# Six transformer layers after a new table of times: a quarter of a layer between the two samples, query shifts in four groups, high and low parts transposed together

## The reference, cut to what matters

```
for i in range(6):
    xn = _adaln(x, noise_emb, n1_w[i], n1_b[i])            # layer norm, gain and shift from the noise embedding
    q, k, v = split(xn @ qkv_w[i].T);  q = _rope(q); k = _rope(k)
    x = x + _attn(q, k, v, src_mask) @ so_w[i].T           # softmax(q k^T / sqrt(8)) v, 512 x 512 per head
    xn = _adaln(x, noise_emb, n2_w[i], n2_b[i])
    q = _rope(xn @ cq_w[i].T); k = _rope(context @ ck_w[i].T); v = context @ cv_w[i].T
    x = x + _attn(q, k, v, ctx_mask) @ co_w[i].T           # 512 x 77 per head
    xn = _adaln(x, noise_emb, n3_w[i], n3_b[i])
    x = x + gelu(xn @ f1_w[i].T + f1_b[i]) @ f2_w[i].T + f2_b[i]
```

## Time and profile before

| | us |
|---|---|
| median of 3 runs (4430.06 to 4431.96) | 4431.53 |
| the profiled execution | 4427.45 |
| its span | 4425.7 |
| of the span: ahead of the six layers | 2869.9 |
| the six layers, first `mean` to last `fres` | 1386.7 |
| behind them | 169.0 |

### The profile page before, as it was taken

How to read it: one execution, slowest core, us unless ns; L and a number is a source line. 1 busy time by engine, 2 the same in 40 slices (tenths; PEclk the granted TensorE clock), 3 DMA queues, 4 the chain that set the end, 5 groups by cost and what they waited for, 6 DMA issues and landing times. The chain is left out here.

```text
span 4425.7 us, 67855 instructions
## 1 busy us (share of the span) xinstructions
PE 3717.7 (84%) x19183; PEld 2083.4 (47%) x19244; DVE 2774.0 (63%) x13500; ACT 2297.4 (52%) x6560; POOL 660.9 (15%) x2307
## 2 busy tenths in 40 slices
PE   7888888888888888888899999678888888888768
PEld 2366667666766666666333333223333333333222
DVE  3457777777777777777544544466666666666534
ACT  5356666666666666666433334135555555555433
POOL 0322222222222222222320000210000000000002
PEclk9999999999999999999999999578888888888879
DMA  0100000000000000000110000011111111111000
GB/s 9 58 1 1 1 1 1 1 2 1 1 1 1 1 1 2 1 1 1 36 38 1 1 1 22 17 59 45 58 47 62 49 61 48 59 46 46 27 27 5
DMA packets 48773, 93.56 MB, mean 21 GB/s; under 512 B 11296, under 2 KB 31792, under 8 KB 48144
## 3 DMA queue, kind: packets, MB, share of 16 engines
q1 hardware_dynamic: 48400, 89.22, 6.2%
HBM read 72.88 MB, written 15.39 MB: 20 GB/s over the span
## 5 line engine op out<-in xcount | busy, mean ns | idle before, releaser
L2250 ACT ACTIVATE t_ex<-ps 128x1024 f32<-128x1024 f32 (+1 forms) x480 | 472.1, 1021 | 572.0 <-PE ps L2197 558.4
L923 PE MATMUL ps<-g_dh,w_p 128*128 128x77 f32 x2032 | 453.0, 304 | 341.0 <-DVE g_dh L1014 341.0
L931 PE MATMUL ps<-g_dh,w_p 128*128 128x128 f32 x4064 | 662.6, 285 | 0.0
L2345 DVE TENSOR_REDUCE t_ncol<-ps 128x1 f32<-128x512 f32 x768 | 486.4, 682 | 157.8 <-PE ps L2170 157.0
L923 PEld LDWEIGHTS ps<-g_dh,w_p 128*128 128x128 f32 x2032 | 302.1, 188 | 535.5 <-DVE g_dh L1014 535.5
L988 DVE SCALAR_TENSOR_TENSOR g_used<-g_encg,g_e 128x77 f32<-128x77 f32 x3072 | 549.7, 229 | 0.0
L931 PEld LDWEIGHTS ps<-g_dh,w_p 128*128 128x128 f32 x4064 | 535.1, 191 | 0.0
L940 PE MATMUL ps<-g_th,g_vrep 128*128 128x77 f32 x2048 | 453.8, 303 | 0.0
L958 ACT ACTIVATE g_th<-ps 128x77 f32<-128x77 f32 x1024 | 242.4, 237 | 400.8 <-PE ps L923 400.8
L935 PE MATMUL ps<-g_dh,g_uhh 128*128 128x129 f32 x2032 | 437.0, 297 | 0.0
L997 DVE TENSOR_REDUCE g_ntop<-ps 128x1 f32<-128x77 f32 x1024 | 243.0, 237 | 260.4 <-PE ps L940 248.3
(11 more groups left out here) (483 smaller groups left out, 5439.1 us busy)
## 6 DMA issues: line engine op xcount, KB each, us to landing
t_qst<-t_turn_q SPq DMA_DIRECT2D x288, 96.0 KB
t_kst<-t_turn_k SPq DMA_DIRECT2D x144, 96.0 KB
t_turn_q<-t_part SPq DMA_DIRECT2D x24, 384.0 KB, 2.5
t_turn_k<-t_part SPq DMA_DIRECT2D x12, 384.0 KB, 3.3
t_wf<-in_t_wf SPq DMA_DIRECT2D x6, 514.5 KB, 5.7
m_experts<-in_experts SPq DMA_DIRECT2D x1, 3072.0 KB, 11.9
t_wa<-in_t_wa SPq DMA_DIRECT2D x6, 448.0 KB, 3.5
t_wx<-in_t_wx SPq DMA_DIRECT2D x6, 448.0 KB, 4.5
```

Source lines behind the costliest of these rows:

```text
L923: M(att[c], w["att_h"], moved(c, t, S), start=False, stop=True, skip_group_check=True).then_inc(*st.sem("att", c))
L931: return M(gates[c][:, g], w["uh"][:, g * D:(g + 1) * D], moved(c, t, SPAN), start=False, stop=False, skip_group_check=True)
L2250: A(ex[0:kw, slot[pf, c, l, n]], ps[0:kw, at:at + 2], ACT.Exp, scale=SCALE).then_inc(*st.sem(f"{pf}e{n}", c))
L2345: V.tensor_reduce(ncol[:, c, n % TT, n // TT:n // TT + 1], ps[:, at], AX, ALU.max, negate=True)\
```

## The change

There are two tables, one for each lane, with new times; a layer is due every 207.24 us and lane 1 comes 52.59 us behind lane 0. High and low parts share a tile (`nhl`), are transposed by one step `tr` and copied by one step `rc`; the shift rows of self attention go in four groups of 4 heads. A reader's time in the choice of PSUM banks is no longer 1.0 us but by its kind, and a slot of `ex` is chosen as the one due free first. Semaphores are kept per lane in two objects. Cut to its core:

```diff
-    LAYER, LAG = 209.87, 104.92
-    TABLE = {
-            "s a": [24.99, 25.21, 25.56, ... 95.17],
-            "s b": [70.18, 71.46, ... 121.77],
-            "x a": [153.28, ... 158.94],   "x res": [188.99],   "f fres": [208.94],
-            "s rows": [66.72, 100.26],
+    LAYER, LAG = 207.24, 52.59
+    TABLE = ({                                # lane 0
+            "s a": [26.5, 27, ... 89.37],
+            "s b": [46.73, 48.47, ... 105.26],
+            "x mean": [115.65],  "x a": [141.35, ... 160.14],  "f mean": [187.69],  "f fres": [206.44],
+            "s kt": [16.1],  "s qt": [17.4],  "s kl": [19.9, 26.2, 30.4, 34.6],  "s ql": [22, 24.1, 28.3, 32.5],
+            "s rows": [43.51, 57.45, 81.13, 93.44],  "load": [58.59],
+        }, {                                  # lane 1
+            "s a": [37.43, 38.99, ... 97.96],
+            "s b": [58.46, 59.18, ... 113.5],
+            "x mean": [125.98],  "x a": [146.84, ... 159.59],  "f mean": [185.21],  "f fres": [204.88],
+            ...
+        })
-        nhi, nlo = sb("nhi", [P, B, TT, H3], BF16), sb("nlo", [P, B, TT, H3], BF16)
-        nrow = sb("nrow", [H3, B, 2, T], BF16)
+        nhl = sb("nhl", [P, B, TT, 2 * H3], BF16)
+        nrow = sb("nrow", [2 * H3, B, 2, T], BF16)
+        HELD = {"m": 0.75, "e": 1.1, "g": 3.4}
-                until[j], holder[j] = when[reader, pf, c, l, rn] + 1.0, (pf + name, c, l)
+                until[j], holder[j] = when[reader, pf, c, l, rn] + HELD.get(reader, 0.8), (pf + name, c, l)
-        slot = {e: i % EXR for i, e in enumerate(exps)}
+        for e in exps:
+            i = min(range(EXR), key=lambda i: slot_until[i])
+            slot[e], slot_held[e] = i, slot_holder[i]
+            slot_until[i], slot_holder[i] = when["o", e[0], e[1], e[2], e[3] // 2] + 1.15, e
-                    sp.wait_ge(*st.at(f"{pf}rhi{n}", c, l))
-                    sp.wait_ge(*st.at(f"{pf}rlo{n}", c, l))
-                    hs = 8 * n if pf == "s" else 0
-                    nh = 8 if pf == "s" else H3
+                    sp.wait_ge(*st[c].at(f"{pf}rc{n}", 0, l))
+                    hs, nh = (4 * n, 4) if pf == "s" else (0, H3)
                     for i in range(2):
-                        sp.dma_start(qst[SHIFT_ROW + i:SHIFT_ROW + i + 1, c, hs:hs + nh], nrow[0:nh, c, i]).then_inc(shifted[pf, c], 16)
+                        sp.dma_start(qst[SHIFT_ROW + i:SHIFT_ROW + i + 1, c, hs:hs + nh], nrow[nh * i:nh * i + nh, c, n % 2])\
+                            .then_inc(shifted[pf, c], 16)
-                elif what in ("thi", "tlo"):
+                elif what == "tr":
+                    pe.wait_ge(*st[c].at(f"{pf}lo{n}", 0, l))
+                    hs, nh = (8 * n, 8) if pf == "s" else (0, 2 * H3)
                     for t in range(TT):
+                        mm = M(ps[0:nh, at, t * P:(t + 1) * P], nhl[:, c, t, hs:hs + nh], identb[:], start=True, stop=True)
-                    if pf == "s" and n % 16 == 0:
-                        pe.wait_ge(shifted["s", c], 16 * (4 * l + 2 * (n // 16) + 2))
+                    if pf == "s" and n % 8 == 0:
+                        pe.wait_ge(shifted["s", c], 16 * (8 * l + 2 * (n // 8) + 2))
                     elif what == "q1":
-                        dve.wait_ge(*st.at(pf + "qr", c, l))
-                        V.tensor_copy(q1, qr).then_inc(*st.sem(pf + "q1", c))
+                        dve.wait_ge(*st[c].at(pf + "qr", 0, l))
+                        V.tensor_copy(q1, qr).then_inc(*st[c].sem(pf + "q1"))
-                    dve.wait_ge(*st.at(f"{pf}m{32 * n + 31 if pf == 's' else H3 // 2 - 1}", c, l))
+                    dve.wait_ge(*st[c].at(f"{pf}m{16 * n + 15 if pf == 's' else H3 // 2 - 1}", 0, l))
+                elif what == "rc":
+                    nh = 8 if pf == "s" else 2 * H3
+                    dve.wait_ge(*st[c].at(f"{pf}tr{n}", 0, l))
+                    if n >= 2:
+                        dve.wait_ge(shifted["s", c], 16 * (8 * l + 2 * (n - 1)))
+                    V.tensor_copy(nrow[0:nh, c, n % 2], ps[0:nh, bank("tr", pf, c, l, n)]).then_inc(*st[c].sem(f"{pf}rc{n}"))
```

More of the change, by code:

```diff
@@ new lines, in transformer3_stage @@
+    LAYER, LAG = 207.24, 52.59
+    TABLE = ({
[34 rows of a table added]
+            },
+            "act": {
+                "s sq": [1.1],
+                "s rstd": [2.88],
+                "s e": [47.45, 49.19, 50.93, 52.66, 54.4, 57.57, 59.31, 63.68, 65.42, 68.22, 71.84, 72.92, 74.66, 76.4, 78.75,
+                    80.49, 85.96, 87.04, 88.12, 89.2, 90.31, 91.86, 92.94, 94.02, 96.9, 97.98, 99.06, 100.14, 101.23, 103.02,
+                    104.1, 105.98],
+                "s og": [82.93, 108.21],
+                "s inv": [84.71, 109.99],
+                "x sq": [116.75],
+                "x rstd": [120.22],
+                "x e": [168.35, 169.43, 170.98, 172.06, 174.28, 175.83, 176.91, 179.2],
+                "x og": [175.25, 181.43],
+                "x inv": [177.95, 183.52],
+                "f sq": [188.79],
+                "f rstd": [190.57],
+                "f g": [197.71],
+            },
+            "dve": {
[36 rows of a table added]
+            },
+            "pool": {
+                "s ks": [9.4],
+                "x ks": [16],
+            },
+            "sp": {
+                "s kt": [16.1],
+                "s qt": [17.4],
+                "s kl": [19.9, 26.2, 30.4, 34.6],
+                "s ql": [22, 24.1, 28.3, 32.5],
+                "x kt": [39],
+                "s rows": [43.51, 57.45, 81.13, 93.44],
+                "x kl": [44.11],
+                "x qt": [133.36],
+                "x ql": [136.56, 141.36, 143.46, 138.66],
+                "x rows": [164.17],
+                "load": [58.59],
+            },
+        }, {
[34 rows of a table added]
+            },
+            "act": {
+                "s sq": [1.1],
+                "s rstd": [3.7],
+                "s e": [59.18, 60.26, 61.41, 63.14, 64.88, 66.6, 69.82, 72.6, 74.34, 76.07, 77.96, 79.7, 81.65, 83.15, 84.23,
+                    86.61, 92.18, 93.94, 95.68, 97.18, 98.92, 100.21, 101.95, 103.24, 106.53, 107.81, 109.12, 110.47, 111.55,
+                    112.63, 113.71, 114.79],
+                "s og": [88.84, 117.81],
+                "s inv": [90.93, 120.44],
+                "x sq": [127.58],
+                "x rstd": [129.65],
+                "x e": [168.49, 169.57, 170.65, 171.73, 172.81, 173.89, 175.44, 176.52],
+                "x og": [174.86, 178.75],
+                "x inv": [177.49, 180.53],
+                "f sq": [186.31],
+                "f rstd": [188.09],
+                "f g": [195.81],
+            },
+            "dve": {
[36 rows of a table added]
+            },
+            "pool": {
+                "s ks": [10.75],
+                "x ks": [19.05],
+            },
+            "sp": {
+                "s kt": [17.45],
+                "s kl": [21.25, 23.35, 26.45, 37.55],
+                "s qt": [25.45],
+                "s ql": [29.15, 31.25, 33.35, 35.45],
+                "x kt": [41.95],
+                "x kl": [46.95],
+                "s rows": [55.34, 68.79, 88.17, 102.59],
+                "x qt": [139.24],
+                "x ql": [142.44, 146.64, 148.74, 144.54],
+                "x rows": [165.17],
+                "load": [58.59],
+            },
+        })
@@ L1990, in transformer3_stage @@
             for c in range(B):
-                for engine, steps in TABLE.items():
+                for engine, steps in TABLE[c].items():
                     for name, times in steps.items():
@@ L2009, in step_names, with lane_steps @@
             return [pf + part for part in parts.get(what, what).split()]
-        def lane_steps(engine):
-            rows = sorted((t, *name.rpartition(" ")[::2], n) for name, times in TABLE[engine].items() for n, t in enumerate(times))
+        def lane_steps(engine, c):
+            rows = sorted((t, *name.rpartition(" ")[::2], n) for name, times in TABLE[c][engine].items() for n, t in enumerate(times))
             return " ".join(name for t, pf, what, n in rows for name in step_names(what, pf, n))
-        st = Steps(k, "t6", 2, pe=lane_steps("pe"), act=lane_steps("act"), dve=lane_steps("dve"), pool=lane_steps("pool"))
+        st = [Steps(k, f"t6_{c}", 1, **{e: lane_steps(e, c) for e in ("pe", "act", "dve", "pool")}) for c in range(B)]
         def bank_use(what, pf, n):
@@ L2140, in _ @@
                     if pf == "s" and l:
-                        pe.wait_ge(*st.at("ffres", c, l - 1))
+                        pe.wait_ge(*st[c].at("ffres", 0, l - 1))
                     elif pf != "s":
-                        pe.wait_ge(*st.at("sres" if pf == "x" else "xres", c, l))
-                    M(ps[:, at], center[:], k.y[:, c], start=True, stop=True).then_inc(*st.sem(pf + "mean", c))
+                        pe.wait_ge(*st[c].at("sres" if pf == "x" else "xres", 0, l))
+                    M(ps[:, at], center[:], k.y[:, c], start=True, stop=True).then_inc(*st[c].sem(pf + "mean"))
```

(33 more changed lines are left out.)

202 lines of the change are left out of this document (77 added, 125 removed), and 213 rows, old and new, of the table TABLE.

## The result

| | before | after |
|---|---|---|
| median of 4 runs, us | 4430.8 (4425.94 to 4431.96) | 4348.36 (4347.19 to 4353.79) |
| ratio, 95% interval | | 0.9818 (0.9801 to 0.9835) |
| the profiled execution | 4427.45 | 4348.47 |
| the six layers, first `mean` to last `fres` | 1386.7 | 1302.7 |

The forecast was 4355 in a range from 4330 to 4400, and the kernel is 82 us faster, where 76 were forecast. The gain lies in the stage: 1386.7 - 1302.7 = 84.0. Between the two profiled executions the rest took 5 us more (3.6 ahead of the stage, 1.4 behind it), though it is the same code. The start of the stage lies between 2867 and 2881 us in the thirteen traces of this case, so times of single executions carry some us that have nothing to do with the stage.

What follows compares the result with a forecast made beforehand. No engine was full; a lane's own chain held the beat, PE nearest its limit and its clock slowed. New stage 6 x 212 + 38.6 = 1310.6 against 1386.7, 76 less: 4351.4, plus 4.1 for the median, 4355; range 4330 to 4400.

Steps and rivals of the forecast that it cites:

- Form of the sum: Six-layer stage: six beats p plus head and tail, 6p + 38.6 in place of 6p + 75.2, 36.6 us less.
- Beat: Steady time p of one layer of both lanes: 218.6 falls to 212 us, bounds 207 and 218.6.
- Rival A: Six layers: new table missed like the old, beat stays 218.6, only the lag pays; 4395 us, chance 18%.
- rival B: Six layers: new table met, beat 207.2, slow clock vanishes; 4327 us, chance 11%.
- The clock, as the reason: PE on lane 0's chain: one fall instead of two, 10 us of slow clock left, adding 5.2 us a beat.
- that for the beat being right but not its reason: Layer's windows: clock not at 0.5 for some 10 us around lane 0's layer end, but elsewhere.
- PE's 169 us at the full clock: PE's work in a layer of both lanes, priced start to start: 169 us; rest of 190.9 busy is slow clock.
- rival C: Six layers: thinly spread PE work keeps the clock low, 0.77, beat 233, slower at 4482 us; chance 6%.
- Banks and slots: Choice of PSUM banks and exponential slots by due time: worth 0, between -1 and +1 us a layer.
- Groups of four: Shift rows: extra `hilo` 0.7 us offset by one 0.67 copy saved; new wait for landings 0, at worst 23 a layer.
- Query casts: Casts already on DVE: beside POOL they make q3 some 3 us late; costs 0, at worst 3 us.
- rival D: The change does nothing it says, as casts were on DVE already; held for casts only, no separate chance given.

Runs made afterwards that it cites:

- the fastest kernel here: Changed kernel, still four groups and a quarter-layer lag, with both tables of times drawn up anew: 4309.97 us, ratio 0.9737 against the kernel before.
- another: Changed kernel with two groups of 8 heads in place of four, quarter-layer lag, tables drawn up anew: 4322.52 us, ratio 0.9766 against the kernel before.
- the 50.0 us offset: Changed kernel with LAG 50.0 in place of 52.59, same tables: 4422.4 us, ratio 0.9997 against the kernel before.
- the groups' 12.6 us: Four against two groups in the changed kernel at quarter-layer lag, each with tables drawn up anew: 4309.97 against 4322.52 us.

## Why the prediction was right

The time came out, and so did the two terms of the sum, but the reason given for the larger one did not. So a good part of it was luck.

**Form of the sum.** 6p + 38.6 was forecast and 6p + 37.9 measured. Of the 84 us, 6 x (218.6 - 210.8) = 46.8 are the beat and 75.2 - 37.9 = 37.3 the lag, for which 36.6 stood. Its parts were wrong. The old head was read from lane 0's row: lane 1's start went from 88.4 to 50.3, 38.1 us and not the 52.3 of the tables, as the old one had been 16.5 ahead of its due time. The first layer went from 4.4 over the beat to 1.4 under it, 5.8 more gained, and the last from 17.6 under it to 11.0, 6.6 lost. I had kept 5 us for a first layer that had not been short before, and 9 for the last. Only their sum, 14 against 52.6 - 37.9 = 14.7, came out.

**From the stage to the time.** The stage was 7.9 us shorter than the 1310.6 of the sum. The rest of the program took 5 us more in this execution, and the 4.1 that I added for the median was not there, as this profile lay on the median of its runs. So the final number is 7 us off, and of these small errors two cancelled in part.

**Beat.** 212 forecast, 210.8 measured. Rival A's 218.6 and rival B's 207.2 both failed. I had said that the new table's prices fit the rows. They do but for one: it leaves 0.86 or 0.87 behind 38 of the 40 `o` of a beat, where the earlier trace rows have 1.00. That is 5.3 us of PE a beat, by this estimate, and may by itself keep the table from being met, full clock or not. But the new table is not a bound of the order: the fastest kernel here is due every 208.6 and comes every 203.2, another is due every 223.3 and comes every 206.5. The due time of a layer is no measure of its beat, and taking 207 as the base was luck as much as reading.

**The clock, as the reason.** This step failed though its size came out. I put the old beat's excess of 8.7 us, and the 5 us kept in the new one, to PE at half clock on lane 0's chain. Raised to 0.96 in the old order, the clock moved no beat. What the change took away is the stretch in which DVE alone had work while ACT stood for 30 us; the clock rose with it, since PE then had `b` and `o` of the other lane to do. The signs I named (clock of 0.93 or more, PE under 190 us busy) were both met, with 0.97 and 184.4, and could not tell the two readings apart: both follow from a denser order. Only doubling PE's work without touching the order could. One sign did speak, that for the beat being right but not its reason: at lane 0's layer end the clock was at half for 3.4 us and not for some 10, and the other three falls of the beat lay elsewhere.

**PE's 169 us at the full clock.** Too low as a busy time: after, at 0.97, PE is busy 184.4. By the groups over the same stretch the `a` of both lanes take 46.4 us, 0.36 each, where I had priced them 0.22 from start to start:
```profile
L2279 PE MATMUL ps<-t_kst,t_qst 96*128 96x512 bf16 x129 | 46.4, 392 | 3.6 <-DVE t_ncol L2453 1.4 <-DMA t_qst<-t_turn_q 0.9 <-DVE x_norm L2406 0.8
```
A product that stands alone is busy for its whole 0.38 or so; only in a row are their starts 0.22 apart. It touched the price of rival C alone.

**Banks and slots.** The step "0, between -1 and +1 a layer" failed: the banks' rule is worth some 20 us, over 3 a layer. Had the old rule been kept, the time would have been 4370, still in the range. The miss is inside a beat that I had guessed 1.2 too long, and so did not show.

**Groups of four.** By their groups over one beat the small steps cost what was reckoned: `hilo` 16 instructions at 0.17, and in cross attention one copy of 0.67 for a lane in place of two:
```profile
L2471 DVE CAST t_nrow<-ps 8x512 bf16<-8x512 f32 x8 | 5.4, 672 | 1.7 <-PE ps L2295 1.5
...
L2465 DVE TENSOR_TENSOR t_nhl<-t_ncol,t_nhl 128x16 bf16<-128x16 f32 x8 | 1.4, 175 | 0.3
L2463 DVE CAST t_nhl<-t_ncol 128x16 bf16<-128x16 f32 x8 | 1.4, 173 | 0.2
L2471 DVE CAST t_nrow<-ps 32x512 bf16<-32x512 f32 x2 | 1.3, 674 | 1.0 <-PE ps L2295 1.0
```
Self attention has eight such copies in both kernels, as one `rc` does the work of `rhi` and `rlo` and there are twice as many. The new wait was nothing, as said. PE's waits over the whole stage, for the landing of the shift rows:
```profile
PE ps L2305 <- DMA t_qst<-t_nrow: 10.7, 6, 3.6
```
That is 1.8 us a layer. With two groups the same wait was 12.5 us over the stage, 2.1 a layer.

**Query casts.** They were on DVE in both kernels, as rival D said, and beside POOL they take what they took the earlier trace rows. The timeline of DVE, and PE's first `a` of the same lane:
```profile
3518.58 1.23 DVE L2434 CAST t_part<-sq 128x512 bf16<-128x512 f32 x1
...
3521.43 1.24 DVE L2440 CAST t_part<-cent 128x512 bf16<-128x512 f32 x1
...
3533.00 0.81 PE L2279 MATMUL ps<-t_kst,t_qst 96*128 96x512 bf16 x3 [0.89 <-DMA t_qst<-t_turn_q]
```
The first `a` waits 0.89 for its stack and comes 27.0 us after the lane's `mean`, due at 26.5: inside the 0 to 3 us I gave it. The last of the cuts ends 17.5 us after the `mean`, where I had reckoned with 19.2.

**The clock as the way to be slower** (rival C). It lacked the size. The clock does fall in several places of a beat, but the four falls of the beat shown end in 3.4 us each, and its mean is 0.97; it would have taken 0.80. The Trainium skill, "TensorE: Matmul & The Clock Gate", on PSUM queue depth-cycling, describes the form of this (a clock that swings as PE pauses between groups). Here it costs 14 us of half clock in a beat against 55 in the two long falls of the old order.

**Left open:** which instances of `a` and `b` stand for their bank first under the old rule, what in the 50.0 us offset collides first, and how much of the groups' 12.6 us is the groups and how much the tables.

## What to carry to other kernels

Where two independent streams share in-order engines, look first for stretches in which one engine is full and another stands for tens of microseconds, and shift the streams until one's full stretch meets the other's need; then draw up the order anew for that shift, since 2.6 us of offset with an unfit order gave back 80 of 84 us. A low clock of PE beside a full DVE can be a symptom, as it was here: double PE's work in that place, and if the time stays, leave the clock alone. Which bank a product gets is part of the order and has a price of its own.

## What the runs showed of the hardware

- 200 more products a beat cost 0.2% and brought the clock from 0.87 to 0.93 and 0.96. They are some 27 us by the earlier trace rows, but PE's busy time in a beat rose only from 191 to 200 and 206, and the beat by 1.6.
- The same instructions in the same order, with other PSUM banks, took 4370 in place of 4353 us.
- A cast of 128x512 to bf16 took 1.23 us on DVE beside POOL, 0.43 on DVE alone, 0.62 on ACT.
- The granted clock fell to 0.5 for 3.4 us at a time in the new order, with PE busy 4.5 of 5 us in the windows at 3370 and 3445 (1.9 and then 4.8 at 3490 and 3495), and for 27.3 us in the old one, with PE busy 3.1 to 4.2 of 5 us in the windows at 0.50.
